# Attention kernel, one core: the row of maxima by a DMA instead of a matmul and a cast, low passes split in two, order of three engines and the late input changed

## The reference

```python
xn = _layernorm(x, axis=-1)
Q = jnp.einsum('bnd,hdk->bhnk', xn, proj_q)
K = jnp.einsum('bmd,dk->bmk', xn, proj_k)
V = jnp.einsum('bmd,dv->bmv', xn, proj_v)
logits = jnp.einsum('bhnk,bmk->bhnm', Q, K)
weights = jax.nn.softmax(logits, axis=-1)
O = jnp.einsum('bhnm,bmv->bhnv', weights, V)
Y = jnp.einsum('bhnv,hdv->bnd', O, proj_o)
mid = jnp.einsum('amh,ehn->aemn', xn, w1)
out = jnp.einsum('aemn,enh->amh', mid, w2)
x = x + Y + out
```

## Time and profile before

| | us |
|---|---|
| median of 3 runs | 1634.11 (1634.03 to 1634.44) |
| the profiled execution, its own time | 1634.65 |
| its span in the profile | 1632.9 |
| PE busy | 1619.3 (99%) |
| DVE, ACT, POOL busy | 1228.6, 1301.2, 1379.2 |

### The profile page before, as it was taken

One profiled execution on the slowest core, in us unless ns is written; L12 is line 12 of the kernel. 1 busy time (PEld: TensorE's weight loads), 2 busy tenths in 40 slices (PEclk: granted clock), 3 DMA queues, 4 the chain that ended last, 5 costly groups with the idle time before them and its releaser, 6 DMA issues. The chain is left out here.

```text
span 1632.9 us, 46345 instructions
## 1 busy us (share of the span) xinstructions
PE 1619.3 (99%) x18710; PEld 1202.5 (74%) x18710; DVE 1228.6 (75%) x2608; ACT 1301.2 (80%) x1349; POOL 1379.2 (84%) x1008
## 2 busy tenths in 40 slices
PE   8999999999999999999999999999999999999998
PEld 6777777777777777777777777777777777777776
DVE  6777777777777777777777777777777777777776
ACT  4688888888888888888888888888888888787786
POOL 3688888888888889888888888888888888888877
PEclk9999999999999999999999999999999999999999
DMA  8000000000000000000000000000000000000000
GB/s 238 4 3 5 5 4 18 4 4 5 3 18 5 4 5 5 16 5 5 4 5 18 3 5 4 4 18 3 5 5 3 18 5 3 4 14 2 2 2 14
DMA packets 34705, 20.41 MB, mean 12 GB/s; under 512 B 18368, under 2 KB 30912, under 8 KB 34496
## 3 DMA queue, kind: packets, MB, share of 16 engines
q1 hardware_dynamic: 33456, 16.92, 3.9%
q10 hardware_dynamic: 1040, 0.52, 0.1%
HBM read 9.57 MB, written 4.19 MB: 8 GB/s over the span
## 5 line engine op out<-in xcount | busy, mean ns | idle before, releaser
L360 POOL TENSOR_TENSOR pr_lo<-pr,pr_hi 128x1024 f16<-128x1024 f32 x511 | 1080.1, 2137 | 227.8 <-ACT pr_hi L463 227.8
L456 ACT ACTIVATE pr<-s_ps,boost,scale 128x1024 f32<-128x1024 f32 x512 | 617.0, 1205 | 193.7 <-PE s_ps L639 193.6
L927 DVE TENSOR_REDUCE key_max<-s_ps 128x128 f16<-128x1024 f32 x512 | 623.9, 1219 | 0.2 <-PE s_ps L624 0.2
L463 ACT ACTIVATE pr_hi<-pr 128x1024 f16<-128x1024 f32 x512 | 525.5, 1051 | 8.1
L637 PE MATMUL s_ps<-g_lo,xT 128*128 128x128 f16 x4096 | 512.4, 219 | 1.0 <-DVE g_lo L940 1.0
L639 PE MATMUL s_ps<-g_hi,xT 128*128 128x128 f16 x4096 | 512.3, 219 | 0.0
L637 PEld LDWEIGHTS s_ps<-g_lo,xT 128*128 128x128 f16 x4096 | 400.7, 98 | 31.4 <-DVE g_lo L940 1.5
L639 PEld LDWEIGHTS s_ps<-g_hi,xT 128*128 128x128 f16 x4096 | 400.8, 98 | 29.9
L679 PE MATMUL t_ps<-pr_hi,xn_hi 128*128 128x512 f16 x1016 | 385.1, 379 | 0.0
L681 PE MATMUL t_ps<-pr_lo,xn_hi 128*128 128x512 f16 x1016 | 385.1, 379 | 0.0
L682 PE MATMUL t_ps<-pr_hi,xn_lo 128*128 128x512 f16 x1016 | 385.1, 379 | 0.0
(11 more groups left out here) (136 smaller groups left out, 1564.1 us busy)
## 6 DMA issues: line engine op xcount, KB each, us to landing
out_dram<-xacc SPq DMA_DIRECT2D x15, 256.0 KB, 2.7
w_sb<-in_L_ffn_w_dram SPq DMA_DIRECT2D x1, 2048.0 KB, 10.0
xT<-xn_hi SPq DMA_TRANSPOSE x56, 2.2
xT<-xn_lo SPq DMA_TRANSPOSE x56, 2.4
pr<-in_L_attn_proj_q_dram ACTq DMA_DIRECT2D x1, 512.0 KB, 4.5
xacc<-in_L_attn_x_dram SPq DMA_DIRECT2D x2, 256.0 KB, 5.1
pr<-in_L_attn_proj_o_dram SPq DMA_DIRECT2D x1, 512.0 KB, 6.7
xacc<-in_L_attn_x_dram SPq DMA_DIRECT2D x1, 384.0 KB, 10.8
```

Source lines behind the costliest of these rows:

```text
L360: pool.tensor_tensor(pr_lo[:, u % RING, :], pr32[:, u % PR, :], pr_hi[:, u % RING, :], ALU.subtract)\
L456: act.activation(pr32[:, u % PR, :], both_banks(u), ACT.Exp, bias=boost[:, 0:1], scale=scale[:, 0:1])\
L463: act.activation(pr_hi[:, u % RING, :], pr32[:, u % PR, :], ACT.Copy).then_inc(p_hi_ready, 1)
L927: dve.tensor_reduce(key_max[:, u % 2, :], both_banks(u).rearrange("p (t q) -> p q t", q=P), AX_X, ALU.max).then_inc(keys_max, 1)
```

## The change

- `minus_max` keeps one column per unit, and a DMA that SP issues (`bias`) writes these 128 float16 elements from 128 partitions into row 0 of g_lo. `max_to_row` and `place_bias` are gone, with rowed and bias_ready; bias_in counts the DMAs. `find_max` waits for the DMA of unit u - 2, which read the same column.
- `low_passes` becomes `low_keys` (xT_lo by g_hi, no bias needed) and `low_queries` (xT_hi by g_lo, waits for bias_in). The first stands before the turn, the second at the end of the iteration; for at = 0 the last 512-column product of the second chunk comes behind it.
- For at = 1 the projection comes before `low_keys`. The first chunk and both halves of the high pass are no longer split by the row matmul.
- DVE: `find_max` comes directly behind `max_of_keys`, ahead of `between_maxima` (scalings, g_low, t_low), except for at = 0.
- ACT: for at = 2 `p_high(n - 2)` comes ahead of `exponentials(n - 1)`.
- SP: a row's DMA per unit; one of 24 loads of two tiles (128 KB) behind each row of units 6 to 29, for the one large load; the two transposes of a tile and the two stores of a batch stand behind rows of different units.

```diff
@@ sync
-            sp.dma_start(xacc[:, 2 * NT:TILES, :], x_tiles[:, 2 * NT:TILES, :]).then_inc(x_in[4], 16)
+            def bias(u):
+                k, j = divmod(u, 4)
+                sp.wait_ge(max_found, u + 1)
+                if j == 0:
+                    sp.wait_ge(g_lo_ready, k + 1)
+                if u >= 1:
+                    sp.wait_ge(bias_in, 16 * u)
+                sp.dma_start(g_lo[0:1, k % 2, j * P:(j + 1) * P], minus_max[:, u % 2:u % 2 + 1]).then_inc(bias_in, 16)
...
+            for u in range(UNITS):
+                bias(u)
+                pair, at = divmod(u, 8)
+                if u in REST:
+                    tile = 2 * NT + 2 * (u - REST[0])
+                    sp.dma_start(xacc[:, tile:tile + 2, :], x_tiles[:, tile:tile + 2, :]).then_inc(x_in[4], 16)
+                if pair == 1 and at in (4, 5, 6, 7):
+                    turn(NT + at // 2 - 2, at % 2)
+                if at in (1, 2) and pair >= 2 and (tile := ln_tile(pair - 2)) is not None:
+                    turn(tile, at - 1)
+                batch = pair // H - 1
+                if pair % H == 2 and at in (5, 6) and batch >= 0:
+                    store(batch, at - 5, 0, HT, 2)
@@ scalar
+                if at == 2 and 2 <= n <= UNITS + 1:
+                    p_high(n - 2)
                 if 1 <= n <= UNITS:
                     exponentials(n - 1)
-                if at == 2 and 2 <= n <= UNITS + 1:
-                    p_high(n - 2)
@@ tensor
                 if n < UNITS:
                     high_pass(n, 0)
-                if 1 <= n <= UNITS and at != 3:
-                    max_to_row(n - 1)
-                if n < UNITS:
                     high_pass(n, 1)
-                if 1 <= n <= UNITS and at == 3:
-                    max_to_row(n - 1)
...
                 chunk(n, 0)
-                small_products(n)
+                if at == 1:
+                    small_products(n)
                 if 1 <= n <= UNITS:
-                    low_passes(n - 1)
+                    low_keys(n - 1)
+                if at != 1:
+                    small_products(n)
                 if at == 2:
-                    chunk(n, 1, rest=False)
+                    chunk(n, 1, (0, 1))
                 if n < UNITS:
                     turn_keys_max(n)
-                chunk(n, 1, first=at != 2)
+                chunk(n, 1, ((0, 1), (0, 1, 2), (2,), (0, 1, 2))[at])
+                if 1 <= n <= UNITS:
+                    low_queries(n - 1)
+                if at == 0:
+                    chunk(n, 1, (2,))
@@ vector
-                if 1 <= n <= UNITS:
-                    place_bias(n - 1)
                 if n < UNITS:
                     max_of_keys(n)
-                between_maxima(n)
+                if n % 4 == 0:
+                    between_maxima(n)
                 if n < UNITS:
                     find_max(n)
+                if n % 4 != 0:
+                    between_maxima(n)
```

More of the change, by code:

```diff
@@ L223, in turned_in @@
             return 32 * (tiles - NT)
+        REST = range(6, 6 + (TILES - 2 * NT) // 2)
         def ln_slot(tile):
@@ L297, in store @@
                 sp.dma_start(out_tiles[:, tile:tile + count, :], xacc[:, tile:tile + count, :]).then_inc(stored, 16)
-            for tile in range(NT, AHEAD):
-                turn(tile)
-            for pair in range(PAIRS):
-                if (tile := ln_tile(pair - 1)) is not None:
-                    turn(tile)
-                if pair >= H + 1 and (pair - H - 1) % H == 0:
-                    for half in range(2):
-                        store((pair - H - 1) // H, half, 0, HT, 2)
+            for u in range(UNITS):
[11 more added lines that the diff above has]
+                    store(batch, at - 5, 0, HT, 2)
             store(B - 1, 0, 0, HT, 2)
@@ L627, in high_pass, with low_keys, low_queries @@
                     last.then_inc(high_done, 1)
-            def low_passes(u):
+            def low_keys(u):
                 k, j = divmod(u, 4)
-                pe.wait_ge(bias_ready, u + 1)
+                pe.wait_ge(keys_max, u + 1)
+                for t in range(NT):
+                    pe.matmul(bank(u, t // HT)[:, (t % HT) * P:(t % HT + 1) * P], x_lo(batch_tile(k) + t),
+                              g_hi[:, k % 2, j * P:(j + 1) * P], start=False, stop=False, skip_group_check=True)
+            def low_queries(u):
+                k, j = divmod(u, 4)
+                pe.wait_ge(bias_in, 16 * (u + 1))
                 if j == 0:
@@ L635, in low_passes @@
                 for t in range(NT):
-                    dst = bank(u, t // HT)[:, (t % HT) * P:(t % HT + 1) * P]
-                    pe.matmul(dst, x_hi(batch_tile(k) + t), g_lo[:, k % 2, j * P:(j + 1) * P],
-                              start=False, stop=False, skip_group_check=True)
-                    last = pe.matmul(dst, x_lo(batch_tile(k) + t), g_hi[:, k % 2, j * P:(j + 1) * P],
-                                     start=False, stop=True, skip_group_check=True)
+                    last = pe.matmul(bank(u, t // HT)[:, (t % HT) * P:(t % HT + 1) * P], x_hi(batch_tile(k) + t),
+                                     g_lo[:, k % 2, j * P:(j + 1) * P], start=False, stop=True, skip_group_check=True)
                 last.then_inc(scores_ready, 1)
@@ L669, in weigh @@
                 dst = sum_bank(k).rearrange("p (j c) -> p j c", j=4)
-                if first:
+                if 0 in products:
                     if t == 0:
@@ L717, in fold_ffn, with chunk @@
                     last.then_inc(f_ps, 1)
-            def chunk(n, place, first=True, rest=True):
-                if n < 4 and rest:
+            def chunk(n, place, products=(0, 1, 2)):
+                if n < 4 and 2 in products:
                     turn_w1(2 * n + place)
-                if n in FOLDS and rest:
+                if n in FOLDS and 2 in products:
                     for e in range(2):
@@ L729, in chunk @@
                 if 0 <= k < LAST:
-                    weigh(k, t, first, rest)
+                    weigh(k, t, products)
             def head_out(k, g):
```

57 lines of the change are left out of this document (22 added, 35 removed).

## The result

The changed kernel takes **1672.15 us** (median of four runs, 1668.18 to 1673.06) against 1634.07 for the kernel before, run alternately with it (1633.67 to 1634.44). The ratio is 1.0228, with a 95% interval from 1.0211 to 1.0246: slower by 38 us, where 1641.5 and at most 1662 were forecast. The sign of being wrong that the forecast named for the DMA, a landing above 2.67 us, is there: 2.78 in the median. The profiled execution took 1668.18 us, the shortest of the four. The four runs lie 4.9 us apart, those of the kernel before 0.8.

A forecast was written before the change was run, and what follows sets the result against it. TensorE (PE), busy 99%, was taken to bound the kernel, so any new wait costs its full length. 1634.65 - 28.5 + 18.3 + 8.5 + 8 + 1 = 1642, as a median 1641.5 us; range 1611 to 1662.

The forecast's parts named there:

- sign of being wrong: For the row's DMA: a landing above 2.67 us would show the prediction wrong; 1.8 to 2.4 was expected.
- removal of 512 row matmuls: On PE: 512 row matmuls at 0.0556 us of spacing go, all on the path, -28.5 us.
- a): Exponential before the projection, n%4 = 1: PE stands still 0.145 us in 126 blocks, +18.3 us.
- b): Maxima over keys before the turn, n%4 = 3 and some 0: PE waits 0.045 in 126 + 63 iterations, +8.5 us.
- c): Second half of the high pass, n%4 = 2, needs the next block's g_lo: 54 waits of 0.15, +8 us.
- d): The row's DMA: taken to land in 1.8 us, under the 2.67 available in the shortest case, so 0.
- e): SyncE's queue of transposes, stores and 24 loads: each 0 while a row's DMA follows 3 us later.
- f): ScalarE's rounding ahead of one exponential: delays it to about 0.1 us before PE needs it, n%4 = 3; 0.
- g): Start and end: first units lack a chunk to cover the DMA, last scores come 0.4 later; +1 us, 0 to +3.
- third rival: Row lands late, g_lo matmuls wait: 1700 at 3.0 us, 1645 to 1660 for a small overlap with b); chance 0.13.
- first rival: Only the wait for the exponential is real, those of b) and c) are not: 1625 us, faster; chance 0.27.
- the second: Rival: PE finds no new wait at all, 1606.6 us, faster; chance 0.10.

The follow-up runs named there:

- e1: The changed kernel without the row's DMA and its waits, scores times 0 in the exponential: 1641.16 us, ratio 1.0044.
- e2: The kernel before without its row matmul and the cast into g_lo, scores times 0 in the exponential: 1613.40 us, ratio 0.9874.
- e3_four_bytes: The changed kernel with the DMA moving 128 elements of 4 bytes into a separate row of one partition, maximum not used in the scores: 1646.32 us.
- e3_two_bytes_column: The changed kernel with the DMA copying 128 elements of 2 bytes into a column over 128 partitions, maximum not used in the scores: 1646.05 us.
- e5: The changed kernel with ScalarE's old order for n%4 = 2, the rounding behind the exponential: 1734.28 us, ratio 1.0614.
- e12: The kernel before without row matmul and cast, with the change's ScalarE order (rounding ahead of the exponential at n mod 4 = 2): 1631.92 us, ratio 0.9987.
- e11: The changed kernel with 4-byte elements in g_lo; for n%4 = 0 one second-chunk product before the turn, two behind the g_lo matmuls: 1632.94 us, ratio 0.9988.
- e7: The changed kernel with the later input in one 3 MB load at the start, not 24 small loads: 1678.53 us, ratio 1.0276.

## Why the prediction was wrong

| step | forecast | measured |
|---|---|---|
| removal of 512 row matmuls | -28.5 | -28.5 (0.056 in each iteration of e1 and e2 that has no wait) |
| a) exponential | 0.145 x 126 = 18.3 | 0.162 x 126 = 20.4 |
| b) maxima over keys | 0.045 x 189 = 8.5 | 0.060 x 189 = 11.3 |
| c) g_lo of the next block | 0.15 x 54 = 8 | 0.029 x 54 = 1.6 |
| d) the row's DMA | 0 | 31.0 by medians, 25.7 as PE's waits in the profiled execution |
| e) SyncE's queue | 0 | 0 |
| f) ScalarE's order | 0 | 0, but 62 without it |
| g) start and end | 1 | about 2 (what is left in e1) |

**The step that failed is d).** It said "I take 1.8, since this is a plain DMA with far fewer bytes". The row lands in 2.78 in the median. The cover that it was set against was right: 2.67 and 2.77 us for turns in n%4 = 2 and 1 are just where the ordinary rows come short, and 2.89 where none does. Only for n%4 = 0, given 2.75, is there more room than that, about 3.0. With 2.78 the third rival's small overlap would have been the case, 1645 to 1660, still short of the measured 1672. The second half of the error is that a median was compared with the cover at all. One row in nine is more than 2.9 us on its way, and these make 15.0 of the 19.6 us from 200 to 1500 us. The transposes had shown such a tail, 2.3 in the median and 4.0 at most; I had kept it as the bound of the landing, and not as a share of the rows with its own price. Of the two halves the landing is the larger. e3_four_bytes and e3_two_bytes_column have late landings too, up to 3.6, but with the rest at 1.6 to 1.9 they take 5 us more than e1_no_row and not 31. These runs, at 1646, lie inside the forecast's range. It is the 2.78, with next to no cover to spare, that makes each late row dear. The chance of 0.13 for the third rival was too low for a transfer of a kind that no row showed, and the range's upper end too near. The rule of the Trainium skill that was weighed there ("DMA: Bandwidth & Descriptors", Rules for kernel authors) names one descriptor per element. The landings agree in direction, 1.6 for one row and 2.8 for 128 elements, but 128 elements to 128 partitions also land in 1.6.

**a) and b)** were the right mechanisms at the right places, each 10 to 30% too small: differences of 1.5 us read to 0.01 or 0.02.

**c)** was oversized. The chain of the same kind, by the timeline at 807 us:

```profile
807.93 0.29 ACT L441 ACTIVATE xn_hi<-xn 128x127 f16<-128x127 f32 x1
...
808.13 0.58 ACT L466 ACTIVATE g_hi<-s_ps 128x512 f16<-128x512 f32 x1
...
808.74 0.69 DVE L940 TENSOR_TENSOR g_lo<-s_ps,g_hi 128x512 f16<-128x512 f32 x1
```

From the split to g_hi are 0.20 us in all 54 places and not the 0.30 of the earlier trace rows. In the kernel before g_hi's input came only then: the projection's last product starts at 815.17 and its recorded 0.38 ends at 815.55, g_hi starts at 815.59. The step between two links was taken from a place where the second one waited for another engine. With 0.20 the chain is 4.02, against 3.97 and the 0.02 by which a) was too small, and this leaves the 0.03 that is measured.

**e)** Rows do follow every 3 us, and neither transposes nor stores show among PE's waits. Of the 470 rows of units 30 to 499 one alone is issued more than 0.15 us after all that it waits for. **f)** was right in its amount and wrong in its weight: "the cover that goes next" is a chain over ScalarE and GpSimd, and e5 and e12 show both of its ends. The first rival (1625) is out by e1, the second (1606.6) by the first view of the waits.

The change removed 28.5 us of work and turned it into 34 us of waits that its own order made, plus 26 to 31 for the row. e11 gets the same work done in 1632.94: with a quick row the exponential's wait can be bought off, and the gain is then still only 1.6 us, since most of the wait for the maxima over keys, the spaced operand and the late rows remain.

## What to carry to other kernels

Where the bound engine has no slack, a matmul on it that is replaced by a transfer buys its own spacing and sells the cover of everything that stood behind it: lay each distance beside its chain, and count a transfer by its distribution, since what a late landing exceeds the cover by is paid in full. Price a transfer of a shape that the trace doesn't have as unknown, and measure it alone before the order is built round it; bytes alone don't rank transfers. And look which engine is next behind the bound one (here GpSimd, 0.15 us behind): it keeps part of any gain, and small reorderings on the engines that feed it can be worth more than the matmuls.

## What the runs showed of the hardware

- Landing of 128 small elements, SBUF to SBUF, issue to semaphore: 2 bytes each into one partition 2.8 us; alone in 4-byte places 2.7; 4 bytes each into one partition 1.9; 2 bytes each into 128 partitions 1.6; 256 bytes as one row 1.6. In all five the last packet is over by 1.32 us after the issue; what differs is the time from there to the semaphore, 1.46, 1.40, 0.57, 0.33 and 0.29 us.
- Late landings: of 470 rows of the changed kernel (units 30 to 499), 191 were under way while a packet of the trace's instruction queues (q8, q14; 0.93 us in the median) was; 54 of these took over 2.9 us, and none of the other 279. In the late rows the row's own last packet is late, 2.1 us after the issue and not 1.3 (median of the 44 whose packets can be told apart), so this is another thing than the slow 2-byte landing. Transposes beside a row made no difference (19 of 155 late, against 35 of 315), nor did stores (1 of 21). That the instruction packets are the cause is not shown, as no run could leave them out. All variants have this tail, 3.5 to 4.5 us at most, but for the 9.3 of e7's first row.
- A row matmul of 128 columns costs PE 0.0556 us of spacing against 219 ns on record; with a moving operand that takes every second 2-byte value it is 0.058.
- The profile credits a wait for two semaphores to the later event it knows: VectorE's maximum appears as released by the DMA 122 times between 200 and 1500 us. All of these start 0.26 us after the turn of the maxima, as the 187 do that are put down to PE, so it was the turn that they waited for.
